# First attention of an audio tower: tanh in 12 chunks with three argument slots instead of 17 groups with four

## The reference, cut to what matters

```python
score = jnp.einsum('bhtsd,d->bhts', jnp.tanh(q[:, :, :, None, :] + k[:, :, None, :, :]), ws) + bs[0]
p_attn = jax.nn.softmax(score, axis=-1)
attn = jnp.einsum('bhts,bhsd->bhtd', p_attn, v)
```

## Time and profile before

| | |
|---|---|
| median of three runs | 1282.94 us |
| the profiled execution | 1281.29 us, of which the span is 1279.6 us |
| busy share of the span | PE 85%, DVE 84%, ACT 78%, POOL 67% |
| first tanh to last tanh begin | 66.8 to 791.3 us |
| stretch 200 to 600 us | ACT 399.85 of 400 us busy, DVE 385.39, POOL 357.75, PE 327.53 |
| the largest single group | tanh (L1031): 272 instructions, 681.3 us |

### The profile page before, as it was taken

One profiled execution on the slowest core, in us unless ns is written; L12 is line 12 of the kernel. 1 busy time (PEld: TensorE's weight loads), 2 busy tenths in 40 slices (PEclk: granted clock), 3 DMA queues, 4 the chain that ended last, 5 costly groups with the idle time before them and its releaser, 6 DMA issues. The chain is left out here.

```text
span 1279.6 us, 44047 instructions
## 1 busy us (share of the span) xinstructions
PE 1081.3 (85%) x18872; PEld 824.9 (64%) x18875; DVE 1072.5 (84%) x2070; ACT 996.7 (78%) x902; POOL 857.4 (67%) x932
## 2 busy tenths in 40 slices
PE   4967878888788788788878877998999999998796
PEld 3644655666566566566656655997567777776595
DVE  8889999999999999999999998588566777788342
ACT  3489999999999999999999999686345555544242
POOL 3099899898889889888988989676011223334354
PEclk9999999999999999999999999998999999999898
DMA  5799999940000000000000000110000200002451
GB/s 161 237 360 359 358 340 330 335 135 11 11 2 11 10 10 4 11 11 2 12 10 3 11 11 3 50 26 1 2 3 3 69 20 19 19 14 62 133 156 45
DMA packets 78547, 107.84 MB, mean 84 GB/s; under 512 B 6963, under 2 KB 76489, under 8 KB 78356
## 3 DMA queue, kind: packets, MB, share of 16 engines
q1 hardware_dynamic: 67894, 91.62, 21.9%
q0 software_dynamic: 5360, 8.02, 2.0%
q10 hardware_dynamic: 5104, 5.43, 1.5%
HBM read 18.32 MB, written 83.85 MB: 80 GB/s over the span
## 5 line engine op out<-in xcount | busy, mean ns | idle before, releaser
L1031 ACT ACTIVATE work<-work 128x2864 f32<-128x2864 f32 (+1 forms) x272 | 681.3, 2598 | 4.9 <-POOL work L452 4.7
L452 POOL TENSOR_TENSOR work<-shared 128x1253 f32<-128x1253 f32 (+1 forms) x272 | 612.1, 2268 | 79.2 <-PE psum L2074 68.0
L2074 PE MATMUL psum<-work,ws_place 128*32 128x179 f32 x8640 | 395.2, 322 | 138.0 <-ACT work L1031 112.9
L452 DVE TENSOR_TENSOR work<-psum,shared 128x1611 f32<-128x1611 f32 (+3 forms) x288 | 488.0, 1722 | 1.0 <-PE psum L2074 0.4
L2074 PEld LDWEIGHTS psum<-work,ws_place 128*32 128x32 f32 x8640 | 269.3, 111 | 229.6 <-ACT work L1031 174.4
L2279 PE MATMUL psum<-shared 32*32 32x179 f32 (+1 forms) x3456 | 99.1, 326 | 1.2 <-DVE peaks L1682 0.7
L1407 DVE SCALAR_TENSOR_TENSOR p_sb<-psum,bs_col,s_top 128x358 f32<-128x358 f32 x144 | 82.1, 570 | 15.0 <-PE psum L2086 0.2
L920 POOL DMA_INDIRECT xs_dram<-w_store,slot_i x24 | 28.5, 1188 | 81.0 <-DVE slot_i L1782 74.8
L2086 PE MATMUL psum<-ident,p_sb 128*128 128x128 f32 x416 | 77.7, 294 | 1.1 <-ACT pt_region L1017 1.1
L1404 DVE TENSOR_REDUCE s_top<-psum 128x2 f32<-128x358 f32 x144 | 71.5, 496 | 5.5 <-PE psum L2074 5.4
L2086 PEld LDWEIGHTS psum<-ident,p_sb 128*128 128x128 f32 x416 | 43.5, 142 | 42.3 <-issue 33.4
(11 more groups left out here) (445 smaller groups left out, 2023.7 us busy)
## 6 DMA issues: line engine op xcount, KB each, us to landing
xs_dram<-pad_row SPq DMA_DIRECT2D x23, 3088.0 KB, 28.6
pt_region<-xs_dram SPq DMA_DIRECT2D x19, 193.0 KB, 2.4
pt_region<-xs_dram ACTq DMA_DIRECT2D x19, 193.0 KB, 2.8
xs_dram<-pad_row SPq DMA_DIRECT2D x1, 2895.0 KB, 28.4
pt_region<-v_sb SPq DMA_DIRECT2D x22, 96.0 KB
work<-in_x SPq DMA_DIRECT2D x2, 768.0 KB, 9.8
work<-in_x ACTq DMA_DIRECT2D x2, 768.0 KB, 12.5
work<-in_L_ffn_W2T SPq DMA_DIRECT2D x1, 1536.0 KB
```

Of the source, the lines that this page charges most:

```text
L452: ins = eng.tensor_tensor(dst[:, a * KEEP:e * KEEP].rearrange("p (u s) -> p u s", s=KEEP), k[:, h * KP:h * KP + KEEP].unsqueeze(1).to_broa ...
L1031: act.activation(a, a, ACT.Tanh).then_inc(tanh_done, 1)
L2074: ins = pe.matmul(bank_s[p % 2][32 * quad:32 * quad + 32, at:at + KEEP], ws_place[:, j, :], arg_slot(n)[:, u * KEEP:(u + 1) * KEEP], start ...
```

## The change

The 270 units are divided into 12 chunks, eight of 24 units, three of 20 and one of 18. Sums, tanh and the scores' wait for the tanh go by chunk, duos and `smax` still by group; a semaphore step (`MARKS`) stands at each chunk's and each group's end. Three slots of 24 units replace four of 16, so that `work` grows from 12288 to 12888 columns; `ctx_rows`, which lay in it, now shares `peaks`, and its blanking moves from the start of GpSimd's program into `later_blanks`. VectorE takes 13 of 24, 11 of 20 and 10 of 18 units. The work that hangs on group g follows the chunk in which group g ends (`GROUPS_OF`): group 13 ends in chunk 9, group 16 in chunk 11, group 1 in chunk 1. In a group the four column blocks now take units u, u+1, u+2, u+3 instead of u, u+4, u+8, u+12, and `context` writes its result with a step of four. The idle products ahead of x_max are 22 + 9 instead of 24 + 9, and the wait for `qv_blank` stands behind them.

```diff
+CHUNK = 24
+SIZES = [24] * 8 + [20] * 3 + [18]
+CHUNKS = len(SIZES)
+FIRSTS = [sum(SIZES[:c]) for c in range(CHUNKS)]
+ENDS = [FIRSTS[c] + SIZES[c] for c in range(CHUNKS)]
+GROUP_ENDS = [min(UG * g + UG, UNITS) for g in range(GROUPS)]
+MARKS = sorted(set(ENDS + GROUP_ENDS))
+GROUPS_OF = [[g for g in range(GROUPS) if FIRSTS[c] < GROUP_ENDS[g] <= ENDS[c]] for c in range(CHUNKS)]
...
-        work = sb("work", [128, 12288])
+        work = sb("work", [128, 3 * CHUNK * KEEP])
...
-        arg_slots = [work[:, n * UG * KEEP:(n + 1) * UG * KEEP] for n in range(4)]
-        ctx_rows = work[:, 4 * UG * KEEP:4 * UG * KEEP + 3 * WIDE].rearrange("p (r t) -> p r t", t=WIDE)
+        arg_slots = [work[:, n * CHUNK * KEEP:(n + 1) * CHUNK * KEEP] for n in range(3)]
...
-        def dve_units(g):
-
-            return 8 if g == GROUPS - 1 else 9
+        def dve_units(c):
+
+            return {24: 13, 20: 11, 18: 10}[SIZES[c]]
...
-            pool.memset(ctx_rows[:, :, :], 0.0)
...
-                need(pool, scored, n - 3)
-                sums(pool, arg_slot(n), k_sb[b % 2], q_cols[b % 2], g, dve_units(g), units(g)).then_inc(args_pool, 1)
+                need(pool, scored, scored_chunk(n - 3))
+                sums(pool, arg_slot(n), k_sb[b % 2], q_cols[b % 2], c, dve_units(c), SIZES[c]).then_inc(args_pool, 1)
...
-                    pool_sums(b, g)
-                    if g == 1 and b + 1 < B:
+                    pool_sums(b, c)
+                    if c == 0 and b + 1 < B:
                         pre_norm(b + 1)
-                    if b < EARLY and g in (4, 6, 8):
-                        spread_v(pool, b, (g - 4) // 2)
+                    if b < EARLY and c in (3, 4, 5):
+                        spread_v(pool, b, c - 3)
...
                 if n == 3:
+                    pool.memset(peaks[:, :, :], 0.0)
...
-                        a = arg_slot(n)[:, 0:units(g) * KEEP]
+                        a = arg_slot(n)[:, 0:SIZES[c] * KEEP]
                         act.activation(a, a, ACT.Tanh).then_inc(tanh_done, 1)
-                    if g in (8, 12, 16) and real(b):
-                        exps(b, (g - 8) // 4)
-                    if g in (3, 4) and real(b - 1):
-                        exps(b - 1, EXPS - 2 + g - 3)
+                    if c in (5, 8, 11) and real(b):
+                        exps(b, (c - 5) // 3)
+                    if c in (2, 3) and real(b - 1):
+                        exps(b - 1, EXPS - 2 + c - 2)
...
+            dve.wait_ge(w1_step, 2)
             for b in range(B + 1):
-                for g in range(GROUPS):
-                    if real(b):
-                        dve_sums(b, g)
+                for c, g in ((c, g) for c in range(CHUNKS) for g in GROUPS_OF[c]):
+                    if real(b) and g == GROUPS_OF[c][0]:
+                        dve_sums(b, c)
                     after_sums(b, g)
...
-            def score_group(b, g):
-                n, p = b * GROUPS + g, b * DUOS + g // 2
-                at = g % 2 * KEEP
+            def score_chunk(b, c):
+                n = b * CHUNKS + c
                 pe.wait_ge(tanh_done, n + 1)
-                if g % 2 == 0:
-                    need(pe, smax_done, p - 1)
-                for j in range(4):
-                    for quad in range(4):
-                        u = 4 * quad + j
...
+                for u in range(FIRSTS[c], ENDS[c]):
+                    g, j, quad = u // UG, u % UG // 4, u % 4
+                    p = b * DUOS + g // 2
+                    at = g % 2 * KEEP
+                    if u % (2 * UG) == 0:
+                        need(pe, smax_done, p - 1)
...
+                    if u + 1 in MARKS:
+                        ins.then_inc(scored, 1)
...
-                                "p (k i c) -> p k i c", i=8, c=4)[:, :, 0:4, :]
+                                "p (k j q) -> p k q j", j=8, q=4)[:, :, :, 0:4]
...
-            pe.wait_ge(qv_blank, 4)
             pe.wait_ge(small1, 2)
             pe.wait_ge(y_step, B - 1)
-            warm_up(24)
+            warm_up(22)
             pe.wait_ge(f_added, B)
             pe.wait_ge(n3_step, B - 2)
             warm_up(9)
             pe.wait_ge(x_maxed, 1)
+            pe.wait_ge(qv_blank, 4)
             pe.transpose(bank_k0[:, 0:128], x_max[:, 0:1].to_broadcast([128, 128]), ident[:, :]).then_inc(x_alled, 1)
```

More of the change, by code:

```diff
@@ L270, in build @@
         peaks = sb("peaks", [128, ROUNDS, 256])
+        ctx_rows = peaks
         peaks_tail = sb("peaks_tail", [128, ROUNDS, TA])
@@ L427, in units, with scored_upto, scored_chunk @@
             return min(UG, UNITS - g * UG)
-        def dve_units(g):
-            return 8 if g == GROUPS - 1 else 9
+        def dve_units(c):
+            return {24: 13, 20: 11, 18: 10}[SIZES[c]]
         def arg_slot(n):
-            return arg_slots[n % 4]
+            return arg_slots[n % 3]
+        def scored_upto(b, unit):
+            return len(MARKS) * b + MARKS.index(unit) + 1
+        def scored_chunk(n):
+            return scored_upto(n // CHUNKS, ENDS[n % CHUNKS]) if n >= 0 else 0
         def pt_bank(k):
@@ L443, in parts @@
         def parts(g, lo, hi):
-            hi = min(hi, units(g))
-            cut = min(max(UA - g * UG, lo), hi)
+            cut = min(max(UA - FIRSTS[g], lo), hi)
             return [(h, a, e) for h, a, e in ((0, lo, cut), (1, cut, hi)) if e > a]
@@ L454, in sums @@
                     k[:, h * KP:h * KP + KEEP].unsqueeze(1).to_broadcast([128, e - a, KEEP]),
-                    q[:, g * UG + a:g * UG + e].unsqueeze(2).to_broadcast([128, e - a, KEEP]), ALU.add)
+                    q[:, FIRSTS[g] + a:FIRSTS[g] + e].unsqueeze(2).to_broadcast([128, e - a, KEEP]), ALU.add)
             return ins
@@ L677, in pre_norm, with pool_sums @@
                 ins.then_inc(normed_ready, 1)
-            def pool_sums(b, g):
-                n = b * GROUPS + g
-                if g == 0:
+            def pool_sums(b, c):
+                n = b * CHUNKS + c
+                if c == 0:
                     pool.wait_ge(q_ready, b + 1)
                     pool.wait_ge(k_ready, b + 1)
-                need(pool, scored, n - 3)
-                sums(pool, arg_slot(n), k_sb[b % 2], q_cols[b % 2], g, dve_units(g), units(g)).then_inc(args_pool, 1)
+                need(pool, scored, scored_chunk(n - 3))
+                sums(pool, arg_slot(n), k_sb[b % 2], q_cols[b % 2], c, dve_units(c), SIZES[c]).then_inc(args_pool, 1)
             NORM_LINKS = 22
@@ L746, in _ @@
             for b in range(B):
-                for g in range(GROUPS):
-                    pool_sums(b, g)
-                    if g == 1 and b + 1 < B:
+                for c in range(CHUNKS):
+                    pool_sums(b, c)
+                    if c == 0 and b + 1 < B:
                         pre_norm(b + 1)
-                    if b < EARLY and g in (4, 6, 8):
-                        spread_v(pool, b, (g - 4) // 2)
+                    if b < EARLY and c in (3, 4, 5):
+                        spread_v(pool, b, c - 3)
                     if b == B - 1:
-                        for n in range(NORM_LINKS * g // GROUPS, NORM_LINKS * (g + 1) // GROUPS):
+                        for n in range(NORM_LINKS * c // CHUNKS, NORM_LINKS * (c + 1) // CHUNKS):
                             norm_link(0, n)
@@ L787, in _ @@
             pool.sem_inc(w1_ready, 1)
-            pool.wait_ge(args_pool, B * GROUPS)
+            pool.wait_ge(args_pool, B * CHUNKS)
             for n in range(NORM_LINKS):
@@ L1391, in pre_v, with dve_sums @@
                 ins.then_inc(v_ready, 1)
[L1393 to L1396, removed]
+            def dve_sums(b, c):
+                n = b * CHUNKS + c
+                need(dve, scored, scored_chunk(n - 3))
+                sums(dve, arg_slot(n), bank_k[b % 2], q_cols[b % 2], c, 0, dve_units(c)).then_inc(args_dve, 1)
             def smax(b, k):
@@ L1402, in smax @@
                 top = s_top[p % 2][:, 0:w]
-                dve.wait_ge(scored, b * GROUPS + 2 * k + w)
+                dve.wait_ge(scored, scored_upto(b, GROUP_ENDS[2 * k + w - 1]))
                 dve.tensor_reduce(top, s, AX.X, ALU.max).then_inc(top_step, 1)
@@ L2062, in pre_v_mm @@
                 ins.then_inc(v_psum, 1)
-            def score_group(b, g):
-                n, p = b * GROUPS + g, b * DUOS + g // 2
-                at = g % 2 * KEEP
+            def score_chunk(b, c):
+                n = b * CHUNKS + c
                 pe.wait_ge(tanh_done, n + 1)
-                if g % 2 == 0:
-                    need(pe, smax_done, p - 1)
-                for j in range(4):
-                    for quad in range(4):
-                        u = 4 * quad + j
[L2073 to L2077, removed]
+                for u in range(FIRSTS[c], ENDS[c]):
[4 more added lines that the diff above has]
+                        need(pe, smax_done, p - 1)
+                    ins = pe.matmul(bank_s[p % 2][32 * quad:32 * quad + 32, at:at + KEEP], ws_place[:, j, :],
```

(10 more changed lines are left out.)

## The result

The kernel after takes **1302.89 us** (median of 4 runs, 1301.92 to 1307.36) against 1283.61 us for the kernel before (1281.63 to 1284.97): ratio 1.0161, 95% interval 1.0149 to 1.0173. It is 19 us slower. The forecast was 1299.8 us within 1284 to 1309. The profiled execution of after is the longest of its four runs, 1307.36 us, span 1305.6 us, mean granted clock 0.956 (before 0.982).

The account below looks back on a forecast made before the run. ScalarE was taken to bound the stage, VectorE close behind. Terms -8.0 + 25.8 + 0.75 + 1.5 + 0.3 - 3.5 = +16.9 us on 1281.29 give 1298.2, as a median 1299.8 us; range 1284 to 1309.

Parts of the forecast that it names:

- Heads, -8.0 us: ScalarE's tanh: five fewer instructions in each of 16 sequences, 80 heads of 0.10 us saved, if ScalarE never waits.
- The end of a sequence, 14 x 1.84 us: Scores, projection, add and next first sums take 8.48 us against 6.64; ScalarE waits 1.84 us at 14 ends, +25.8 us.
- the turned duo: Exponentials after the last tanh need duo 5 turned by TensorE: 1.14 us late, lying inside the longer wait.
- GpSimd, 0.75 us: `pre_norm` between GpSimd's two first sums makes chunk 1 0.75 us late; shows only at sequence 0's end, +0.75 us.
- Start and end: Stage start, GpSimd's second sums before the third tanh: +1.5 us; stage end, last scores of 18 units for 14: +0.3 us.
- Slots, 0: Three slots for four: a sum waits for scores three chunks before; needs 9.4 of 11.0 us, so costs nothing.
- Idle products, -3.5 us: Ahead of x_max: with the wait moved behind the idle products, its transpose starts at 897.8 for 901.31, -3.5 us.
- Context, 0: `context` writing in steps of four: at most +1.1 us from the score's pass, which TensorE has room for; taken as 0.
- the rival: Slow context: passes in steps of four cost 0.05 us each, turned duo 1 late after chunk 5; 1312 us, chance 0.06.
- The step that failed: Sequence end: chunk 9's longer scores +0.30 us, a wait between ready groups +0.17, TensorE's times taken from rows of before.
- a VectorE that is half a microsecond late: Upper bound at a sequence's end: VectorE not ready when the projection is, wait 2.3 us, 32 us in all.

Follow-up runs that it names:

- experiment 3: Kernel after with v made after group 12, the projection's add after group 3 of the next sequence, `pre_norm` after chunk 2: 1277.35 us, 0.9949 of before.
- experiment 1: Kernel after with VectorE's add of the projection moved behind the first sums of the next sequence: 1295.55 us, ratio to before 1.0094.
- experiment 4: Kernel of experiment 3 with `pre_norm` after chunk 0 again: 1290.8 us, ratio to before 1.0055.
- experiment 7: Kernel of experiment 3 with 28 and 16 idle products where TensorE waits around a sequence's end: 1278.09 us, beside 1277.48 without them.
- Experiment 6: Kernel after with idle products at sequence ends, 16 behind group 12's scores and 28 behind the last turned duo: 1300.17 us, ratio to before 1.0133.

## Why the prediction was right

- **Heads, -8.0 us: right.** 0.50 us a sequence was worked out from the earlier trace rows; without the waits the period is 0.48 us shorter (experiment 3).
- **The end of a sequence, 14 x 1.84 us: right in place and size.** It is 1.75 us each where the clock stays up. The chain, counted as before from 436.62 + 3.08 = 439.70, is 448.01 - 439.70 = 8.31 us for 8.48; 40 passes are 1.72 us for 1.73. VectorE was idle 1.15 us when the projection came: it was not itself late. Taking the add away (experiment 1) leaves 45.93 - 44.90 = 1.03 us for the turned duo, forecast as 1.14.
- **GpSimd, 0.75 us: right.** 0.70 us at the end of sequence 0, and 0.82 us a sequence once the other chains are away (experiment 4).
- **Start and end: nearly.** Up to the first mark the terms give 1.5 + 0.75 - 0.50 = 1.75 us, measured 2.3; from the fifteenth to the last mark -0.50 + 0.3 = -0.2, measured -0.9. Neither was taken apart.
- **Slots, 0: right.** Experiment 3 keeps three and reaches 44.90 us with no wait in the middle of a usual sequence.
- **Idle products, -3.5 us: right.** From the last mark to x_max's transpose it is 105.30 us before and 101.73 after, -3.57, though the last y product in front of it ran at 1.98 us for 1.16.
- **Context, 0: right.** The groups by shape between 100 us and the end of the stage, first of after, then of before:

```profile
L2121 PE MATMUL psum<-pt_region 128*32 128x96 f32 x480 | 17.0, 248 | 0.0
...
L2121 PE MATMUL psum<-pt_region 128*32 128x48 f32 x480 | 12.0, 207 | 0.6 <-issue 0.6
```

```profile
L2105 PE MATMUL psum<-pt_region 128*32 128x96 f32 x480 | 17.3, 247 | 0.0
...
L2105 PE MATMUL psum<-pt_region 128*32 128x48 f32 x480 | 12.6, 207 | 1.9 <-issue 1.9
```

A product into steps of four takes 248 and 207 ns; one into runs of 16 in a row took 247 and 207. The Trainium skill (Advanced Engine Details and Errata, PSUM Cachelines) says that a pattern in PSUM that is not contiguous slows matmuls significantly; for these products the measurement says no, and the rival falls. The Trainium skill (Perfetto Trace Analysis, Optimizing Scalar/DVE Operations) says that grouping into larger operations can improve throughput where the engine is saturated; the trace bears out the head, 0.10 us each. What 80 heads gave, 8 us, is a third of what the ends took.

**What the prediction left out.** The sum gave 1298.2 us for the profiled execution, which took 1307.36; 1299.8 for the median, which is 1302.89. Up to the last mark the terms make 20.4 us, measured 29.8. The step that failed is the one that priced TensorE's part of the chain with rows of before, where the clock was 1.00. The larger chunks leave TensorE idle for 1.7 to 2.5 us in front of chunk 9's scores (before 1.36), and where the clock then falls, scores and projection take longer in a chain that has no slack (2.66 us for 1.72 and 1.01 for 0.59 at 391 us). Of 240 stretches of 3 us from 66 to 786 us the granted clock is under 0.85 in 9 before, 36 after, 17 with idle products in after, and 3 in experiment 7. Experiment 6 prices it at 2.7 us by medians and 6.7 us by the profiled executions; of the 4.9 us of excess left there, 4.5 lie in the first four periods, under the fill. That the time stayed in the range is in part luck: the range reached up to 1309 to hold a VectorE that is half a microsecond late, which did not happen, and the clock's share fitted into that room.

## What to carry to other kernels

Merging work of a saturated engine into larger pieces pays a head for each piece saved, but it also takes pieces away from behind the work that is hung on them by number: before making chunks larger, count in microseconds what is left behind the last dependent step (here 6.64 us for a chain of 8.48), and move the hand-over first. Where several chains end at the same place, removing one shows the next; here three had to move before ScalarE kept its pace, and then the gain did not show in the time. Where a chain has no slack left, the clock of the engine that only waits in it belongs into its price.

## What the hardware did that was not expected

TensorE is not the bound of this stage, yet its clock lengthens it: with waits of about 2 us in front of short bursts the granted clock fell to 0.50 to 0.56 in stretches of 3 us, and 48 score passes took 3.81 us for 2.03. Idle products in these waits took most of it away: of the 240 stretches of 3 us 15 were under 0.85 in experiment 3, and 3 in experiment 7. They gained nothing in the time there; the longest period that was left, 48.53 us, stood under the fill.

While DMAs of 3 MB ran, at 300 to 360 GB/s, TensorE stopped for up to 2.5 us between two of its products with no semaphore to wait for, in every kernel of this study; moving these DMAs moved the stops. All 48 stops end 1.2 to 1.6 us after a 16 KB packet of the DMA queue of kind "instruction" has arrived.
